# One-core decoder kernel: score order and copies in layer 3 cross attention, layer 0 FFN in chunks of four tiles, layer 2 routing in chunks

## The chip, the cores and the metric

The kernel runs on one core of a Trainium2 chip. The metric is the device time of one execution in microseconds (us), the median of several executions. The engines are TensorE (PE; its weight loads are shown as PEld), VectorE (DVE), ScalarE (ACT), GpSimd (POOL) and the queue of SyncE (SP).

## The reference

Four decoder layers, each of them self attention, cross attention and a feed forward part (FFN), each added to the residual x of 8 x 256 tokens by 128 features after a layer norm. The three parts that matter here:

```python
# layer 0 FFN
gate = jnp.einsum('bsd,hd->bsh', x, wg)      # 384 hidden features
up = jnp.einsum('bsd,hd->bsh', x, wu)
h = jax.nn.silu(gate) * up
return jnp.einsum('bsh,dh->bsd', h, wd)
...
# layer 2 FFN: 16 experts, two per token, 320 places in each
probs = jax.nn.sigmoid(xf @ gate_w.T)
top_vals, sel = jax.lax.top_k(probs, 2)
weights = top_vals / (top_vals.sum(-1, keepdims=True) + 1e-06)
flat_sel = sel.reshape(-1)
onehot = jax.nn.one_hot(flat_sel, 16, dtype=jnp.int32)
ranks = jnp.take_along_axis(jnp.cumsum(onehot, axis=0), flat_sel[:, None], axis=1)[:, 0] - 1
valid = ranks < capacity
slot = jnp.where(valid, flat_sel * capacity + ranks, sentinel)
padded = jnp.zeros((sentinel + 1, d), xf.dtype).at[slot].set(x_rep)
...
# layer 3 cross attention: q is the normalised x, k and v are the context, 16 heads of 8 features
scores = jnp.einsum('bhqd,bhkd->bhqk', qh, kh) + encoder_attention_mask
weights = jax.nn.softmax(scores, axis=-1)
ctx = jnp.einsum('bhqk,bhkd->bhqd', weights, vh)
return jax.nn.relu(ctx @ wo_w.T + wo_b)
```

## The kernel before

The residual lies in SBUF as 16 tiles of 128 tokens (NT = 16, two tiles per batch, TPB = 2, B = 8 batches). The stages follow one another in the order of the layers. A stage is a block: each engine runs its own list of instructions, written out by hand in program order, and waits on semaphores for the others. No engine enters the next block before all have left the last one. Nothing reorders the lists, so the order of the code sets the order of the work. All arithmetic is float32.

**Layer 0 FFN** is two blocks. `normalize_and_turn` (names L0n_...) is a loop over the 8 batches: DVE normalises two tiles into the one buffer `h`, PE transposes them into `psT`, ACT copies them to `part` and again to `hT`. `layernorm_scales` in front of it loads ACT's table and makes 1/std. `experts` (names L0f_...) is a loop over the 8 batches: PE multiplies gate and up weights with 256 tokens, two of the three blocks of 128 hidden features into one pair of PSUM banks and the third into another; ACT applies silu, DVE multiplies (`hidden`), PE multiplies with the down weights (`down`), DVE adds to x and takes the statistics for the next layer norm (`take_stats`).

**Layer 2 FFN** is three blocks. `turn_and_route` normalises in chunks of four tiles, transposes, and makes 16 logits per token. `slots_of_two` (names L2r_...) makes of all 16 tiles at once the sigmoid, the two best experts (`first_best`, twice), the count of tokens ahead of each (PE multiplies `count` with a triangular matrix and with ones; a chain of 15 small additions adds the tiles up in `ahead`) and the row number (`slot`) of each token and choice. `slot_experts` (names L2f_...) begins with 32 indirect DMAs from POOL's queue, two for each tile, that scatter the rows into the DRAM buffer `packed`; SP waits for all 32 and then loads the rows of the first pair of experts.

**Layer 3 cross attention** is `masked_heads` (names L3x_...). Its unit is an item: two heads times 128 queries times 256 keys, 16 items per batch, 128 in all. Four items are a group, and share one `score`: four products, one in each of four row strips of PE, into the four banks psS. Per item, DVE adds the mask and takes the row maximum (`reduce`, two instructions with a readout each), ACT takes the exponential (`exponent`, two instructions), PE transposes four 128x128 blocks into one of the two banks psE (`turn_exp`), and ACT or DVE copies them out (`keep`), as `by_dve(i)` says: every fourth by DVE. At the end of a batch PE multiplies with v (`weigh`, four parts), and in the next batch's items follow `keep_raw` (ACT), `spread_sums` (PE, row sums), `invert` (ACT, Ln and Exp), `divide` (POOL), `project` (PE) and `settle_x` (DVE). `score(g+1)` stands on PE before the transposes of the fourth item of group g (r == 3). `turn_exp(i)` waits for the copy of item i-2. On ACT the copy of item i-2 follows the exponential of item i.

## Time and profile before

| | |
|---|---|
| median of the timed executions | 1830.55 us (two others: 1828.64 and 4648.13) |
| the profiled execution | 1822.58 us, of which the span of the trace is 1820.9 us |
| PE busy | 1421.6 us, 78% |
| DVE busy | 851.2 us, 47% |
| ACT busy | 774.2 us, 43% |
| POOL busy | 430.0 us, 24% |
| mean granted TensorE clock | 0.899 of 2.4 GHz |

The busy shares are means over stages that differ much. The trace's times run from the start of the span. The three stages of the change lie at 416 to 490 us (layer 0 FFN), 1230 to 1405 us (layer 2 FFN) and 1451 to 1697 us (layer 3 cross attention). A float32 product shows as two MATMUL instructions in the trace, and a transpose as one.

### The profile page before, as it was taken

The page shows a single profiled execution, that of the slowest core. Times are in us where ns is not written, and L with a number is a line of the kernel's source. Part 1 is how long each engine was busy: PE and PEld are TensorE (multiplying, and loading weights), DVE is VectorE, ACT ScalarE, POOL GpSimd, SP SyncE. Part 2 cuts the span into 40 slices and gives each one's busy share as a digit, 9 for nine tenths or more (in the row PEclk, how much of TensorE's full clock was granted, in tenths as well). Part 3 has the DMA queues.
Part 4 walks back from the last instruction along what each step waited for, and adds up shares of the span by engine and source line. Part 5 has one row for each costly group of instructions (what it writes and reads, how often), then busy time and mean ns, then how long its engine had stood idle before and what let it go on. Part 6 is the DMA issues. An engine that isn't in the chain of part 4 may idle for free. (4 is left out here: it accounts for less than half of the span.)

```text
span 1820.9 us, 28110 instructions
## 1 busy us (share of the span) xinstructions
PE 1421.6 (78%) x10037; PEld 796.7 (44%) x10037; DVE 851.2 (47%) x2388; ACT 774.2 (43%) x1655; POOL 430.0 (24%) x512
## 2 busy tenths in 40 slices
PE   6899999994699999886997999872182668777585
PEld 4344444443544444464465344362161534344364
DVE  4555555533345655455113665354033545455432
ACT  3244444442167677551430233442020476767233
POOL 5543333300022110100003433001553222220034
PEclk9999999997999999896999999985596898898787
DMA  7900000000000000000004000000222000000022
GB/s 211 120 1 2 2 1 1 1 2 0 0 1 1 1 1 1 1 1 1 1 1 171 1 2 1 1 1 8 76 59 68 13 7 13 7 13 1 4 61 74
DMA packets 60253, 42.29 MB, mean 23 GB/s; under 512 B 13189, under 2 KB 54121, under 8 KB 60121
## 3 DMA queue, kind: packets, MB, share of 16 engines
q1 hardware_dynamic: 54752, 32.42, 7.2%
q0 software_dynamic: 3552, 7.33, 1.2%
q8 instruction: 80, 1.31, 0.3%
q10 hardware_dynamic: 1816, 0.81, 0.2%
q14 instruction: 53, 0.43, 0.1%
HBM read 25.88 MB, written 14.66 MB: 22 GB/s over the span
## 5 line engine op out<-in xcount | busy, mean ns | idle before, releaser
L927 ACT ACTIVATE L0a_probs<-L0a_psL 128x512 f32<-128x512 f32 x192 | 104.2, 594 | 203.5 <-PE L0a_psL L735 73.5
L1313 ACT ACTIVATE L3x_e<-L3x_e,L3x_neg_max 128x256 f32<-128x256 f32 x256 | 116.1, 504 | 69.0 <-DVE L3x_neg_max L1366 69.0
L1229 PE MATMUL L3x_psE<-ident,L3x_e 128*128 128x128 f32 x512 | 91.5, 308 | 61.5 <-ACT scores_L_experts_L L1321 59.3
L991 DVE TENSOR_REDUCE L0a_mx_part<-L0a_psS 128x4 f32<-128x512 f32 x120 | 77.3, 686 | 106.1 <-PE L0a_psS L678 81.8
L1366 DVE CUSTOM_DVE_ANT_0 L3x_e<-L3x_psS,L3x_mask_rows 128x256 f32<-128x256 f32 x256 | 90.9, 421 | 65.1 <-PE L3x_psS L1221 65.1
L1229 PEld LDWEIGHTS L3x_psE<-ident,L3x_e 128*128 128x128 f32 x512 | 61.5, 155 | 119.7 <-ACT L3x_e L1313 86.1
L580 POOL TENSOR_SCALAR L0a_km<-L0a_kT,quad_rows 128x256 f32<-128x256 f32 x64 | 58.4, 930 | 198.9 <-ACT L0a_kT L898 198.9
L670 PE MATMUL L0a_psS<-L0a_km,L0a_qT 32*128 32x512 f32 x360 | 102.2, 644 | 0.2 <-DVE L0a_mx_part L996 0.2
L927 ACT ACTIVATE L2a_probs<-L2a_psL 128x512 f32<-128x512 f32 x96 | 52.1, 594 | 104.2 <-PE L2a_psL L731 69.4
L704 PE MATMUL L0a_psL<-L0a_qm,L0a_kT 32*128 32x512 f32 x256 | 72.9, 643 | 21.8 <-DVE L0a_mx L991 20.3
L1565 PE MATMUL L1a_psL<-L1a_soft_near,neg_tri 128*128 128x512 f32 x128 | 67.9, 612 | 0.2 <-DVE L1a_soft_near L1772 0.2
L2847 POOL DMA_INDIRECT packed_rows<-h,slot x32 | 31.0, 967 | 142.8 <-POOLq L92 133.3
L1772 DVE TENSOR_TENSOR L1a_soft_near<-L1a_soft_near,L1a_psL 128x512 f32<-128x512 f32 x64 | 41.1, 684 | 41.4 <-ACT L1a_soft_near L1702 41.4
L1728 ACT ACTIVATE scores_L_experts_L<-L1a_psL 128x512 f32<-128x512 f32 x96 | 53.5, 594 | 12.8 <-PE L1a_psL L1569 12.8
L580 POOL TENSOR_SCALAR L0a_qm<-L0a_qT,quad_rows 128x256 f32<-128x256 f32 x64 | 58.0, 924 | 0.0
L1469 POOL TENSOR_SCALAR L1a_qm<-L1a_qT,quad_rows 128x256 f32<-128x256 f32 x32 | 29.0, 925 | 113.1 <-ACT L1a_qT L1683 113.1
L1321 ACT COPY scores_L_experts_L<-L3x_psE 128x512 f32<-128x512 f32 x96 | 54.6, 569 | 0.2 <-PE L3x_psE L1229 0.2
L991 DVE TENSOR_REDUCE L2a_mx_part<-L2a_psS 128x4 f32<-128x512 f32 x56 | 36.1, 686 | 35.7 <-PE L2a_psS L678 17.9
L991 DVE TENSOR_REDUCE L0a_mx<-L0a_psS 128x4 f32<-128x512 f32 x60 | 38.6, 685 | 29.2 <-PE L0a_psN L766 26.6
L2881 PE MATMUL L2f_psX<-ident,L2f_rows 128*128 128x128 f32 x40 | 6.9, 311 | 56.6 <-DMA L2f_rows<-packed_rows 55.4
L1163 POOL TENSOR_SCALAR L3x_km<-ctx_T,quad_rows 128x256 f32<-128x256 f32 x32 | 29.1, 925 | 89.3 <-POOLq L92 57.6
L2935 ACT ACTIVATE L2f_hidden<-L2f_psU 128x320 f32<-128x320 f32 x32 | 13.5, 437 | 85.1 <-PE L2f_psU L2891 68.9
(720 smaller groups left out, 3534.6 us busy)
## 6 DMA issues: line engine op xcount, KB each, us to landing
L2f_rows<-packed_rows SPq DMA_DIRECT2D x8, 325.0 KB
packed_rows<-zeros SPq DMA_DIRECT2D x1, 2560.0 KB, 27.8
experts_L_L<-in_L_ffn_w_dram SPq DMA_DIRECT2D x1, 2048.0 KB, 8.7
unpacked_rows<-zeros SPq DMA_DIRECT2D x1, 2048.0 KB, 17.7
scores_L_experts_L<-in_L_ffn_w_dram SPq DMA_DIRECT2D x1, 2048.0 KB, 8.2
L2f_back_rows<-unpacked_rows SPq DMA_DIRECT2D x16, 128.0 KB, 2.5
L3x_mask_rows<-in_mask_Bx1xSxS_ff_dram SPq DMA_DIRECT2D x8, 256.0 KB, 2.7
sorted_rows<-zeros SPq DMA_DIRECT2D x1, 1472.0 KB, 17.6
```

Source lines behind the costliest of these rows:

```text
L580: last = nc.gpsimd.tensor_scalar(dst[:, b % 3, j, :], src[:, b % 3, :], w["rows4"][:, j:j + 1], None, ALU.mult)
L670: last = nc.tensor.matmul(psS[a][:], qT[rows, b % 3, t * P:(t + 1) * P], km[rows, b % 3, :, u * P:(u + 1) * P], start=True, stop=of(b).mas ...
L704: nc.tensor.matmul(bank[:], kT[rows, b % 3, 0:P], qm[rows, b % 3, 2 * k:2 * k + 2, :], start=True, stop=False, skip_group_check=True)
L927: nc.scalar.activation(probs[:, half, a, k, :], psL[i % RING][:], ACT.Exp, scale=scale).then_inc(s_prob, 1)
L991: nc.vector.tensor_reduce(dst, psS[a][:].rearrange("p (j n) -> p j n", j=4), AX.X, ALU.max).then_inc(s_red, 1)
L1229: last = nc.tensor.transpose(psE[i % 2][:, c * P:(c + 1) * P], e[:, i % RING, c * P:(c + 1) * P], mem.ident[:])
L1313: last = nc.scalar.activation(at, at, ACT.Exp, bias=neg[:, i % RING, j:j + 1], scale=-1.0)
L1321: nc.scalar.copy(kept_at(i), turned(i)).then_inc(s_kept_act, 1)
L1366: last = nc.vector.tensor_tensor_reduce(out=e[:, i % RING, j * S:(j + 1) * S], in0=psS[r][:, j * S:(j + 1) * S], in1=mrow[:, b % 2, t, :], ...
L1565: last = nc.tensor.matmul(bank(s, a)[:], w["neg_tri"][:], soft(s, a), start=False, stop=kk == 0, skip_group_check=True)
L1728: nc.scalar.activation(probs[:, half, a, (kk + 2) % 3, :], bank(s, a)[:], ACT.Exp).then_inc(s_prob, 1)
L1772: nc.vector.tensor_tensor(soft(s, a), soft(s, a), bank(s, a)[:], ALU.max).then_inc(s_soft, 1)
```

## The change

In `masked_heads`, `score(g+1)` moves before the transposes of the third item (r == 2), which puts it also before the `weigh` that stands there. DVE copies every second item: item 4g+1 after the reduce of item 4g+3 as before, and item 4g+3 after the reduce of item 4g+4. `settle_x` moves from behind the last reduce of a batch to ahead of it (n == 14). `spread_sums` and `project` write psO in place of psM, and the waits change with that: the next batch's `weigh` waits for `settle_x`.

Layer 0's FFN is one block, `gated_ffn`, written out, with chunks of four tiles (512 tokens): every product has 512 columns, one block of hidden features per pair of banks, two normalised chunks ahead, and the down product of chunk c-1 between the products of chunk c. The wait for the late weights goes.

Layer 2's `turn_and_route` and `slots_of_two` become one block, `send_to_slots`, with chunks of four tiles, and the scatters move into it: POOL sends the eight scatters of a chunk as soon as its slots are ready. SP still waits for all 32, in the next block.

```diff
-        def by_dve(i):
-            return i % 4 == 1
-
         def wait_kept(eng, i):
-            if by_dve(i):
-                eng.wait_ge(s_kept_dve, i // 4 + 1)
+            if i % 2 == 1:
+                eng.wait_ge(s_kept_dve, i // 2 + 1)
             else:
-                eng.wait_ge(s_kept_act, i // 4 * 3 + (1, 0, 2, 3)[i % 4])
+                eng.wait_ge(s_kept_act, i // 2 + 1)
...
-                    if b >= 3:
-                        pe.wait_ge(s_ln, b - 2)
...
                     if r == 0:
                         if b >= 1:
-                            pe.wait_ge(s_raw, b)
+                            pe.wait_ge(s_x, b)
                         else:
                             pe.wait_ge(s_rows_kept, 1)
...
                 def spread_sums(b):
                     pe.wait_ge(s_raw, b + 1)
-                    pe.wait_ge(s_hT, min(b + 3, B))
-                    if b >= 1:
-                        pe.wait_ge(s_x, b)
-                    nc.tensor.matmul(psM[:], w["spread"][:], raw[:], start=True, stop=True).then_inc(s_den, 1)
+                    nc.tensor.matmul(psO[:], w["spread"][:], raw[:], start=True, stop=True).then_inc(s_den, 1)
 
                 def project(b):
                     pe.wait_ge(s_yT, b + 1)
-                    pe.wait_ge(s_hT, min(b + 4, B))
                     for t in range(TPB):
                         for a in range(2):
-                            last = nc.tensor.matmul(psM[:, t * P:(t + 1) * P], yT[:, a, t * P:(t + 1) * P], wo_rows[:, a, :],
+                            last = nc.tensor.matmul(psO[:, t * P:(t + 1) * P], yT[:, a, t * P:(t + 1) * P], wo_rows[:, a, :],
                                                     start=a == 0, stop=a == 1)
...
                         i = ITEMS * b + n
                         g, r = divmod(n, 4)
-                        if r == 3 and i + 1 < LAST:
+                        if r == 2 and i + 2 < LAST:
                             score(i // 4 + 1)
                         if n == 0 and b > 0:
...
                     exponent(i)
-                    if i >= 2 and not by_dve(i - 2):
+                    if i >= 2 and i % 2 == 0:
                         keep(i - 2)
...
                 keep(LAST - 2)
-                keep(LAST - 1)
...
                     reduce(i)
+                    if n % 4 == 0 and i > 0:
+                        keep(i - 1)
                     if n % 4 == 3:
                         keep(i - 2)
-                    if n == 15 and b > 0:
+                    if n == 14 and b > 0:
                         settle_x(b - 1)
+                keep(LAST - 1)
                 settle_x(B - 1)
 
...
+def gated_ffn(nc, mem, w, name, gate, up, down):
...
+                def expand(c, f):
+                    u = PARTS * c + f
+                    if f == 0:
+                        pe.wait_ge(s_hT, c + 1)
+                    if u >= 2:
+                        pe.wait_ge(s_hid, u - 1)
+                    at = slice(c * WIDE, (c + 1) * WIDE)
+                    nc.tensor.matmul(psG[u % 2][:], gate[:, f * P:(f + 1) * P], hT[:, at], start=True, stop=True)
+                    nc.tensor.matmul(psU[u % 2][:], up[:, f * P:(f + 1) * P], hT[:, at], start=True, stop=True).then_inc(s_up, 1)
+
+                def contract(c, tiles_of):
+                    pe.wait_ge(s_hid, PARTS * (c + 1))
+                    if c >= 2:
+                        pe.wait_ge(s_x, c - 1)
+                    for t in tiles_of:
+                        for f in range(PARTS):
+                            last = nc.tensor.matmul(psY[c % 2][:, t * D:(t + 1) * D], hid[:, c % 2, f, t * P:(t + 1) * P], down[:, f, :],
+                                                    start=f == 0, stop=f == PARTS - 1)
+                    if tiles_of[-1] == CHUNK - 1:
+                        last.then_inc(s_down, 1)
+
+                turn(0)
+                turn(1)
+                for c in range(CHUNKS + 1):
+                    if c < CHUNKS:
+                        expand(c, 0)
+                        expand(c, 1)
+                    if c >= 1:
+                        contract(c - 1, (0, 1))
+                    if c < CHUNKS:
+                        expand(c, 2)
+                    if c >= 1:
+                        contract(c - 1, (2, 3))
+                    if c + 2 < CHUNKS:
+                        turn(c + 2)
...
+                normal(0)
+                normal(1)
+                for c in range(CHUNKS + 1):
+                    if c < CHUNKS:
+                        hidden(c)
+                    if c + 2 < CHUNKS:
+                        normal(c + 2)
+                    if c >= 1:
+                        add(c - 1)
...
+def send_to_slots(nc, mem, w, name, gate, rows, packed, scattered, E, capacity):
...
+                for c in range(CHUNKS):
+                    pool.wait_ge(s_twin, c + 1)
+                    pool.wait_ge(s_slot, c + 1)
+                    for t in range(c * CHUNK, (c + 1) * CHUNK):
+                        for i in range(2):
+                            nc.gpsimd.indirect_dma_start(packed, bass.IndirectOffsetOnAxis(ap=slot[:, i, t:t + 1], axis=0),
+                                                         rows[:, i, t, :], None).then_inc(scattered, 16)
...
+                def rank_rows(c):
+                    pe.wait_ge(s_count, c + 1)
+                    if c >= 2:
+                        pe.wait_ge(s_slot, c - 1)
+                    nc.tensor.matmul(psK[c % 2][:, 0:CHUNK * E], w["earlier"][:], count[:], start=True, stop=True)
+                    nc.tensor.matmul(psK[c % 2][:, CHUNK * E:2 * CHUNK * E], w["ones"][:], count[:], start=True, stop=True).then_inc(s_ranked, 1)
+
+                route(0)
+                for c in range(CHUNKS):
+                    if c + 1 < CHUNKS:
+                        route(c + 1)
+                    rank_rows(c)
...
+                def choose(c):
+                    dve.wait_ge(s_exp, c + 1)
+                    steps.step(nc.vector.tensor_scalar(probs[:], probs[:], 1.0, None, ALU.add))
+                    steps.step(nc.vector.reciprocal(probs[:], probs[:]))
+                    best(probs, 0)
+                    steps.step(nc.vector.scalar_tensor_tensor(rest[:], one[:, 0, :, :], -2.0, probs[:], ALU.mult, ALU.add))
+                    best(rest, 1)
+                    if c >= 1:
+                        dve.wait_ge(s_ranked, c)
+                    nc.vector.tensor_tensor(count[:], one[:, 0, :, :], one[:, 1, :, :], ALU.add).then_inc(s_count, 1)
+                    steps.step(nc.vector.scalar_tensor_tensor(total[:], val[:, 0, :], 1e-6, val[:, 1, :], ALU.add, ALU.add))
+                    steps.step(nc.vector.reciprocal(total[:], total[:]))
+                    steps.step(nc.vector.tensor_tensor(val[:], val[:], total[:].unsqueeze(1).to_broadcast([P, 2, CHUNK]), ALU.mult))
...
+                def place(c):
+                    dve.wait_ge(s_ranked, c + 1)
+                    earlier = psK[c % 2][:, 0:CHUNK * E].rearrange("p (t e) -> p t e", e=E)
+                    counts = psK[c % 2][:, CHUNK * E:2 * CHUNK * E].rearrange("p (t e) -> p t e", e=E)
+                    for k in range(CHUNK):
+                        t = c * CHUNK + k
+                        steps.step(nc.vector.tensor_tensor(ahead[:, t + 1, :], ahead[:, t, :], counts[:, k, :], ALU.add))
+                    steps.step(nc.vector.tensor_tensor(equal[:], ahead[:, tiles(c), :], earlier, ALU.add))
+                    steps.step(nc.vector.tensor_tensor(both[:], one[:], equal[:].unsqueeze(1).to_broadcast([P, 2, CHUNK, E]), ALU.mult))
+                    steps.step(nc.vector.tensor_reduce(rank[:].unsqueeze(3), both[:], AX.X, ALU.add))
...
+                steps.step(nc.vector.memset(ahead[:, 0, :], 0.0))
+                normal(0)
+                normal(1)
+                for c in range(CHUNKS):
+                    choose(c)
+                    if c + 2 < CHUNKS:
+                        normal(c + 2)
+                    place(c)
...
-                pool.wait_ge(w["zeroed"], 16 * len(blanks(w)))
-                for t in range(NT):
-                    for i in range(2):
-                        nc.gpsimd.indirect_dma_start(packed, bass.IndirectOffsetOnAxis(ap=slot[:, i, t:t + 1], axis=0),
-                                                     rows[:, i, t, :], None).then_inc(s_scatter, 16)
...
-                sp.wait_ge(s_scatter, 16 * 2 * NT)
+                sp.wait_ge(scattered, 16 * 2 * NT)
...
-        with nc.sbuf_tensor("hT0", [P, NT * P], F32) as hT:
-            normalize_and_turn(nc, mem, w, "L0n", hT)
-            experts(nc, mem, w, "L0f", [(hT, w["L0_ffn_w_gate"][:], w["L0_ffn_w_up"][:], w["L0_ffn_w_down"][:], None)], ACT.Silu)
+        gated_ffn(nc, mem, w, "L0f", w["L0_ffn_w_gate"], w["L0_ffn_w_up"], w["L0_ffn_w_down"])
```

What stands in a row, in three places. First layer 0's FFN on PE. Before, the loop's body for one batch:

```order
L2354 MATMUL L0f_psG<-hT,wT_L_gate 128x256 x2
L2354 MATMUL L0f_psU<-hT,wT_L_up 128x256 x2
L2348 REGISTER_ALU
L2354 MATMUL L0f_psG<-hT,wT_L_gate 128x256
L2354 MATMUL L0f_psU<-hT,wT_L_up 128x256
L2335 REGISTER_ALU
L2336 REGISTER_ALU
L2340 MATMUL L0f_psY<-wT_L_down,L0f_hidden 128x128 x6
```

and now, from the third chunk's transposes on, one chunk's share (L2182 transposes, L2192 and L2193 are gate and up, L2201 is the down product):

```order
L2182 MATMUL L0f_psT<-ident,L0f_h 128x128 x4
L2192 MATMUL L0f_psG<-L0f_hT,wT_L_gate 128x512
L2193 MATMUL L0f_psU<-L0f_hT,wT_L_up 128x512
L2192 MATMUL L0f_psG<-L0f_hT,wT_L_gate 128x512
L2193 MATMUL L0f_psU<-L0f_hT,wT_L_up 128x512
L2201 MATMUL L0f_psY<-wT_L_down,L0f_hidden 128x128 x6
L2192 MATMUL L0f_psG<-L0f_hT,wT_L_gate 128x512
L2193 MATMUL L0f_psU<-L0f_hT,wT_L_up 128x512
L2201 MATMUL L0f_psY<-wT_L_down,L0f_hidden 128x128 x6
```

The products have 512 columns where they had 256, and the down product stands behind the products of the chunk after it.

Second, layer 2's routing on PE. Before, the last two chunks' transposes and logits and the ranking of all 16 tiles (psR of L2r):

```order
L2475 MATMUL L2n_psT<-ident,h 128x128 x4
L2484 MATMUL L2n_psR<-wT_r,L2n_hT 128x16 x8
L2445 UNCONDITIONAL_BRANCH
L2767 UNCONDITIONAL_BRANCH
L2770 MATMUL L2r_psR<-L2r_count,earlier 128x256
L2771 MATMUL L2r_psR<-L2r_count,ones 128x256
```

and now the first two chunks' transposes and logits, the ranking of the first chunk (psK), and the third chunk's:

```order
L2660 MATMUL L2n_psT<-ident,h 128x128 x4
L2665 MATMUL L2n_psR<-wT_r,L2n_hT 128x16 x4
L2660 MATMUL L2n_psT<-ident,h 128x128 x4
L2665 MATMUL L2n_psR<-wT_r,L2n_hT 128x16 x4
L2672 MATMUL L2n_psK<-L2n_count,earlier 128x64
L2673 MATMUL L2n_psK<-L2n_count,ones 128x64
L2660 MATMUL L2n_psT<-ident,h 128x128 x4
```

The ranking stands behind each chunk, with 64 columns, and no longer behind all of them, with 256.

Third, layer 3's cross attention on PE, two groups of a batch. Before (L1221 is score, L1229 the transposes, four for an item, L1208 the next q, L1260 project):

```order
L1221 MATMUL L3x_psS<-L3x_km,L3x_qT 128x512 x4
L1229 MATMUL L3x_psE<-ident,L3x_e 128x128 x4
L1208 MATMUL L3x_psM<-ident,L3x_h 128x128 x2
L1229 MATMUL L3x_psE<-ident,L3x_e 128x128 x12
L1221 MATMUL L3x_psS<-L3x_km,L3x_qT 128x512 x4
L1229 MATMUL L3x_psE<-ident,L3x_e 128x128 x4
L1260 MATMUL L3x_psM<-L3x_wo_rows,L3x_yT 128x128 x4
L1229 MATMUL L3x_psE<-ident,L3x_e 128x128 x12
L1221 MATMUL L3x_psS<-L3x_km,L3x_qT 128x512 x4
```

and now (L1174 is score, L1182 the transposes, L1161 the next q, L1209 project):

```order
L1174 MATMUL L3x_psS<-L3x_km,L3x_qT 128x512 x4
L1182 MATMUL L3x_psE<-ident,L3x_e 128x128 x8
L1161 MATMUL L3x_psM<-ident,L3x_h 128x128 x2
L1182 MATMUL L3x_psE<-ident,L3x_e 128x128 x8
L1174 MATMUL L3x_psS<-L3x_km,L3x_qT 128x512 x4
L1182 MATMUL L3x_psE<-ident,L3x_e 128x128 x8
L1209 MATMUL L3x_psO<-L3x_wo_rows,L3x_yT 128x128 x4
L1182 MATMUL L3x_psE<-ident,L3x_e 128x128 x8
L1174 MATMUL L3x_psS<-L3x_km,L3x_qT 128x512 x4
```

The score moved up past the transposes of one item. On DVE in the same place, the reduces of a group with the copy before (two ISA rows are half an item):

```order
L1366 ISA L3x_e,L3x_neg_max<-L3x_psS,L3x_mask_rows 128x256
L1366 ISA L3x_neg_max 128x1
L1366 ISA L3x_e,L3x_neg_max<-L3x_psS,L3x_mask_rows 128x256
L1366 ISA L3x_neg_max 128x1
L1366 ISA L3x_e,L3x_neg_max<-L3x_psS,L3x_mask_rows 128x256
L1366 ISA L3x_neg_max 128x1
L1376 COPY scores_L_experts_L<-L3x_psE 128x4x128
L1366 ISA L3x_e,L3x_neg_max<-L3x_psS,L3x_mask_rows 128x256
L1366 ISA L3x_neg_max 128x1
```

and now:

```order
L1314 ISA L3x_e,L3x_neg_max<-L3x_psS,L3x_mask_rows 128x256
L1314 ISA L3x_neg_max 128x1
L1324 COPY scores_L_experts_L<-L3x_psE 128x4x128
L1314 ISA L3x_e,L3x_neg_max<-L3x_psS,L3x_mask_rows 128x256
L1314 ISA L3x_neg_max 128x1
L1314 ISA L3x_e,L3x_neg_max<-L3x_psS,L3x_mask_rows 128x256
L1314 ISA L3x_neg_max 128x1
L1324 COPY scores_L_experts_L<-L3x_psE 128x4x128
L1314 ISA L3x_e,L3x_neg_max<-L3x_psS,L3x_mask_rows 128x256
L1314 ISA L3x_neg_max 128x1
```

A second copy (L1324) stands behind the first reduce of each group.

## Rows read from the trace of the kernel before

**Rows 1.** Windows: length; busy us (instructions) of PE, PEld, DVE, ACT, POOL; clock; DMA; GB/s.
```profile
416.00:437.00 21.00, 5.28 (x16) 2.32 (x16) 6.81 (x16) 8.02 (x19) 0.00 (x0) 0.50 0.00 0
437.00:490.00 53.00, 35.32 (x192) 29.61 (x192) 20.52 (x64) 9.13 (x17) 0.00 (x0) 0.95 0.00 0
1230.00:1267.00 37.00, 12.44 (x52) 11.03 (x52) 21.46 (x65) 8.54 (x14) 0.00 (x0) 0.50 0.00 0
1267.00:1309.00 42.00, 0.00 (x0) 0.00 (x0) 0.00 (x0) 0.66 (x1) 30.95 (x32) 0.50 0.15 51
...
1451.00:1697.00 246.00, 180.89 (x1374) 102.29 (x1374) 123.85 (x586) 167.00 (x384) 48.48 (x61) 0.89 0.03 7
```

**Rows 2.** Timeline, layer 0 FFN's normalise stage: start, us, engine, what; [idle before].
```profile
416.05 1.28 ACT L128 ACT_TABLE_LOAD   x1 [4.32 <-PEq L92]
...
435.97 0.40 ACT L2289 COPY hT<-L0n_hT_part 128x256 f32 x1 [0.19 <-ACT L0n_hT_part L2286]
```

**Rows 3.** Timeline, layer 0 FFN, its last batch.
```profile
481.81 1.03 PE L2354 MATMUL L0f_psU<-hT,wT_L_up 128*128 x4
...
484.24 1.02 DVE L2408 TENSOR_TENSOR L0f_hidden<-L0f_activated,L0f_psU 128x512 f32<-128x512 f32 x2 [0.50 <-ACT L0f_activated L2375]
...
485.50 1.58 PE L2340 MATMUL L0f_psY<-wT_L_down,L0f_hidden 128*128 128x128 f32 x12 [1.80 <-DVE L0f_hidden L2408]
...
489.53 0.17 DVE L154 COPY mean_var<-bn_aggr 128x4 f32 x1 [0.24 <-DVE bn_aggr L152]
```

**Rows 4.** Timeline, layer 1 attention: one product with 512 columns, full clock.
```profile
571.50 1.02 PE L1565 MATMUL L1a_psL<-L1a_soft_near,neg_tri 128*128 128x512 f32 x2
```

**Rows 5.** Timeline, layer 2 routing and the first load behind it.
```profile
1232.75 0.69 DVE L2465 TENSOR_TENSOR h<-h,rstd 128x512 f32<-128x512 f32 x1 [1.15 <-ACT rstd L2451]
...
1235.73 1.73 PE L2484 MATMUL L2n_psR<-wT_r,L2n_hT 128*128 128x16 f32 x8
...
1247.32 1.75 DVE L2778 RECIPROCAL L2r_probs<-L2r_probs 128x256 f32<-128x256 f32 x1
...
1254.14 0.42 DVE L2782 TENSOR_TENSOR L2r_count<-L2r_onehot 128x256 f32<-128x256 f32 x1
...
1254.62 1.22 PE L2770 MATMUL L2r_psR<-L2r_count,earlier 128*128 128x256 f32 x2 [10.54 <-DVE L2r_count L2782]
...
1262.90 0.17 DVE L2806 TENSOR_SCALAR slot<-L2r_at 128x16 uint32<-128x16 f32 x1
...
1308.94 7.68 SPq L2861 DMA_DIRECT2D L2f_rows<-packed_rows  x5
```

**Rows 6.** The 32 scatters into packed_rows: ns min/median/max, first and last start.
```profile
L2847 POOL DMA_INDIRECT packed_rows<-h,slot x32: 957/962/1173, 1267.1 to 1306.6; - x32
```

**Rows 7.** Timeline, layer 3 routing: a DVE product beside a scatter.
```profile
1724.77 2.49 DVE L3268 TENSOR_TENSOR h<-h,L3f_score 128x512 f32<-128x512 f32 x4
1726.29 1.30 POOL L3059 DMA_INDIRECT sorted_rows<-h,L3f_slot  x1 [30.44 <-DVE h L3268]
```

**Rows 8.** Layer 3 cross attention grouped by line: busy, mean ns, idle before.
```profile
L1313 ACT ACTIVATE L3x_e<-L3x_e,L3x_neg_max 128x256 f32<-128x256 f32 x256 | 116.1, 504 | 69.0 <-DVE L3x_neg_max L1366 69.0
...
L1321 ACT COPY scores_L_experts_L<-L3x_psE 128x512 f32<-128x512 f32 x96 | 54.6, 569 | 0.2 <-PE L3x_psE L1229 0.2
...
L1376 DVE COPY scores_L_experts_L<-L3x_psE 128x512 f32<-128x512 f32 x32 | 22.1, 692 | 54.6 <-PE L3x_psE L1229 54.6
```

**Rows 9.** The score products of layer 3 cross attention.
```profile
L1221 PE MATMUL L3x_psS<-L3x_km,L3x_qT x256: 587/692/1218, 1451.2 to 1680.8; 32*128 32x512 f32 x128
```

**Rows 10.** Timeline, one group of four items and the next score.
```profile
1546.32 1.14 PE L1221 MATMUL L3x_psS<-L3x_km,L3x_qT 32*128 32x512 f32 x8
...
1547.62 0.42 DVE L1366 CUSTOM_DVE_ANT_0 L3x_e<-L3x_psS,L3x_mask_rows 128x256 f32<-128x256 f32 x1 [2.08 <-PE L3x_psS L1221]
...
1548.43 0.91 ACT L1313 ACTIVATE L3x_e<-L3x_e,L3x_neg_max 128x256 f32<-128x256 f32 x2 [2.62 <-DVE L3x_neg_max L1366]
...
1554.01 1.18 PE L1221 MATMUL L3x_psS<-L3x_km,L3x_qT 32*128 32x512 f32 x8
```

405 lines of the change are left out of this document (148 added, 257 removed).

## The prediction

> **What bounds the kernel now.** I read the windows by stage first, because the shares of the whole span mix stages with different limits, then the timeline inside each stage, and last the grouped lines of the cross attention. [rows 1] is to show that in none of the three stages an engine is full. In layer 0's first 21 us PE is busy for 5.3 and ACT for 8.0; each loop step is a chain of DVE, PE, ACT with nothing beside it, and the granted clock is 0.50, the 1.2 GHz level. In the 53 us behind it PE is busy for 35.3 at 0.95. In layer 2, 37 us pass in which DVE is busy for 21.5 and POOL not at all, and then 42 us in which only POOL works: the 32 scatters go out one after another, from 1267.1 to 1306.6 [rows 6], which is 39.5/31 = 1.27 us each, and nobody else has work. In the cross attention PE is busy for 181 of 246 us, ACT for 167, DVE for 124. There the grouped lines show 69.0 us in which ACT waited for DVE's reduces [rows 8], and a group's timeline shows why: score at 1546.32, first reduce at 1547.62, first exponential at 1548.43, with 2.62 us idle ahead of it [rows 10]. So ACT and DVE sit idle at each group's start because PE begins the score late. All three stages lie on the path to the end, since blocks follow one another.
>
> **Layer 0 FFN.** Now it takes from 416.05 [rows 2] to 489.7 [rows 3], 73.65 us. I lay the new block out. The table load (1.28), Ln and Exp end at about 417.9; one normalising product over four tiles is 0.69 [rows 5], so the first chunk is ready at 418.7. Four transposes take about 1.1 at half clock, two chunks of them until 421.3, the second chunk's normalising keeping pace. One product of 512 columns is two instructions in 1.02 with about 0.17 of pipe [rows 4], so 0.85 in a row, and a gate and up pair 1.7. The first pair runs at half clock (3.0 with the change of clock in it), the others at 1.7: the first chunk is through at 428. From there PE's work in a chunk is three pairs (5.1), twelve down products (two times 1.4, from 1.58 for six [rows 3] less the pipe) and four transposes (0.6): 8.5 us. There is one new wait. DVE normalises chunk c+2 only behind the last `hidden` of chunk c, and PE's transposes of c+2 stand ahead of the next pair: silu 0.6 and its hop 0.2, product 0.7 and normalising 1.4 make 2.9 to 3.3 after the third pair, of which the down products cover 1.3 where there are any. That costs 3.2 us once and 1.9 once. The last chunks need 8.5 each, and the tail (down products, sum, statistics of four tiles) some 4 us. The end comes at about 464.6, so **this part gives 25 us**. It can't be more than 30 (PE's work alone, 34, with start and tail 9), and if the first two chunks stay at half clock, which costs 5 more, it is 20. DVE (about 5.8 per chunk) and ACT (2.4) are hidden below PE. If that cover went, DVE would be next; it has 2.7 us left per chunk.
>
> **Layer 2 routing.** The path to the first load at 1308.94 [rows 5] is: everything for all tiles, then all scatters. In the new block the first chunk is normalised by 1233.44 as now, its logits need transposes and half of the eight instructions' 1.73 and a copy [rows 5], so the exponential ends at about 1237.4. DVE's operations for 64 elements lie between 0.17 (16 elements) and 0.42 (256) [rows 5]; by the line between these about 0.22, with the step 0.26. `choose` is 13 of them, a reciprocal (1.75 for 256, about 0.55 for 64) and three tiny ones: 4.6. PE's ranking (1.22 and 1.06 for 256 columns now) is hidden by the 1.4 of the next chunk's normalising. `place` is four tiny additions and about nine small steps: 2.9. The first slots are there at about 1246.3, where now the first scatter starts at 1267.1. From there the scatters decide: 8 x 1.27 = 10.1 us per chunk, and DVE needs 4.6 + 1.4 + 2.9 = 8.9 for the next. With 32 in a row the last one ends at 1287.2, 20.3 us earlier. SP's wait for them stands now behind the end of a block, which costs 1.7 after the last scatter (as between the last slot and the first scatter now) in place of 1.4: **20 us gained**. The bound above is 21. For the bound below I price 64 elements like 256: DVE then needs 15 us per chunk and is the bound, the last slots come at 1295 and the scatters end at 1305, which leaves 3. I take the first, since the small operations' own rows lie near it. ACT's second copy of the rows and the table load for Gelu, 1.28, now wait for the block's end, but the load and the transposes of 3 us and more cover it.
>
> Here a contention is thinkable, since DVE now works beside the scatters. In the trace a DVE product with both inputs in SBUF (four of them, 2.49 us in all, three steps of 0.60 and one of 0.69) runs beside a scatter that starts at 1726.29 [rows 7], and none of the four is longer than without one. The Trainium skill says in "SBUF — State Buffer", section "Who interferes with whom", that such an instruction contends with a GpSimd instruction that reads SBUF, and that one of the two then blocks for the whole instruction. By that rule some 18 of this gain's 20 us would go (the second rival prices it) and the sum be 51 in place of 69; by the row nothing goes, and I go by the row.
>
> **Layer 3 cross attention.** 32 scores start between 1451.2 and 1680 [rows 9], so a group takes 7.4 us. The cycle without extras: score to first reduce 1.30, reduce to exponential 0.81 [rows 10], three items on ACT of 1.28 each (0.81 exponential, 0.47 copy), 0.1, then the transposes of the third item 0.57 and the next score: 6.6. With the batch's extras (weigh on PE, the copies, Ln and Exp on ACT) such a layout gives 27.9 per batch of four groups, where the trace has 29.6; the difference I put to stretches at half clock, the mean being 0.89 [rows 1]. After the change the third exponential is no longer in the way, and one copy of two has left ACT. The new cycle goes through DVE: score 1.07, transposes of the two items left over 1.14, then DVE's copy of the fourth item 0.69 [rows 8], which stands ahead of the second reduce, the reduce 0.81, the exponential 0.93, the transposes 0.57: 5.3 with the hops. The wait for all four reduces stands in the same place: 1.3 + 0.69 x 5 = 4.8 after the score, and later when the copy waited. In the group of `settle_x` it stands ahead of the last reduce and adds 1.9, to 7.2. The extras of PE and ACT add about 1 us to each of the other three. A batch is then 6.3 + 6.3 + 6.3 + 7.2 = 26.1, the first, without extras, 20.5. That would be 7 x 3.5 + 7.2 = 32 us gained, if the half clock went away; with its present loss of 1.7 per batch it is 19. PE is denser afterwards, so I take a value between, **24 us**. The bounds are 8 (waits for copies eat most of it) and 35. Off ACT go 32 copies of 0.57 [rows 8], onto DVE come 32 of 0.69, 22 us in all; DVE's 124 of 246 become about 146 of 222 and stay hidden. The psO in place of psM removes waits that came early, and costs nothing: `settle_x` is done a group before the `weigh` that waits for it.
>
> **The sum** is 25 + 20 + 24 = 69 us. The profiled execution took 1822.6 with its span of 1820.9, and 1822.6 - 69 = 1753.6. The timed ones have a median of 1830.5, 8 us above it, and the forecast is made for that: **1761.5 us**, 3.8% faster. Since DMA in these stages is light, I expect nothing given back later.
>
> **The rivals.** *First: the new wait eats the earlier score.* The score can't start before the group's four reduces, and DVE now has two copies and `settle_x` among them, each waiting on PE. If the group stays at 7.4, the cross attention gives nothing: 1830.5 - 45 = 1785.5. For it: DVE waited 54.6 us for its present 32 copies [rows 8]. Against it: these waits fell where DVE had no reduce to do.
> *Second: contention in layer 2.* Some 18 of DVE's operations per chunk have two inputs in SBUF. If each waited 0.4 us on average for a scatter (0.96 busy in 1.27), DVE's chunk would take 16 us against 10.1, three times, and 18 of the 20 us are lost: 1779.5. The Trainium skill's rule above speaks for it, [rows 7] against it.
> *Third, and slower than before: the clock.* PE's 181 busy us in the cross attention at 0.89 are 322 at 0.50 [rows 1], 76 more than the 246 it has. If PE stood at the 1.2 GHz level through the stage, it would lose that and the whole be 1830.5 - 45 + 76 = 1861. It decides from a mean clock of about 0.65 there, at which PE's need alone (161 / 0.65) passes 246, and from 0.55 (161 / 0.55 = 293) it outweighs the other 45. Against it: PE's work is packed closer, and 0.89 is far off.
> *Fourth: the change does more than forecast.* With no half clock in the cross attention and 28 from layer 0 it is 1830.5 - 28 - 21 - 33 = 1748.5.
>
> **How the numbers follow.** The forecast, with its own range of 1752 to 1775, gets 0.62; the first rival 0.14; the second 0.04; the third 0.01; the fourth 0.13; what is left, 0.06, is several shortfalls at once. A measurement here tells about 2%, 37 us, from no change, so faster than 1794 counts as faster. The range reaches from the fourth (with 6 us for the scatter between executions, 1742) to the first (1787); outside lie the third, the mixtures, and the half of the first in which other terms fall short too, about 0.14. Faster by over 2%: 0.96. Within 2%: 0.03, a shortfall of two parts at once. Slower: 0.01.
>
> **What the new profile would show.** Layer 0's stage some 48 us long, PE's clock at 1 from its first chunk on, PE waiting twice for the normalising. The first scatter at about 16 us after the block's start instead of 36, 32 scatters without a gap over 0.4 us between chunks, and DVE's 64-element steps near 0.22. Score starts 6.3 to 6.6 us apart, 7.2 in the group with `settle_x`, ACT's wait for reduces well below 69 us, and a clock above 0.89. What would make me wrong is a period of over 7 us, gaps between the scatters' chunks, or PE at half clock through layer 0.

## The result and the profile after

The changed kernel took a median of 1762.2 us (four executions, 1759.7 to 1763.1) where the kernel before took 1830.7 (1828.6 to 1830.8, and one execution of 4648.1 that no ratio uses), a ratio of 0.9627 with a 95% interval of 0.9608 to 0.9646: 68.5 us less, 3.7% faster. Its profiled execution took 1761.7 us with a span of 1760.0, at a mean clock of 0.908.

The forecast was 1761.5 us, 0.7 off. But the two profiled executions are only 60.9 us apart, where I had summed 69. The profiled execution of the kernel before lay 8 us below its median, that of the changed one 0.5 below. So the sum fell 8 us short of what the profiles show, and my adding 8 us back covered that by luck. By block, between the loads of ACT's table that begin them: layer 0's FFN went from 74.5 to 47.6 (27.0 gained, forecast 25); layer 2's FFN from 175.3 to 161.4 (13.9, forecast 20); layer 3's cross attention from 255.0 to 230.7 (24.3, forecast 24); and the unchanged stages between layers 1 and 2 together 3.9 us longer, which I had at nothing.

The windows of the changed kernel by stage (length; busy us of PE, PEld, DVE, ACT, POOL; clock; DMA share; GB/s), for [rows 1]:

```profile
415.63:431.80 16.17, 10.60 (x27) 5.59 (x28) 6.04 (x9) 6.64 (x10) 0.00 (x0) 0.71 0.00 0
431.80:463.20 31.40, 26.46 (x135) 17.75 (x133) 15.16 (x47) 5.97 (x10) 0.00 (x0) 0.99 0.00 1
1207.40:1223.50 16.10, 9.91 (x40) 8.35 (x40) 11.20 (x40) 5.55 (x11) 0.24 (x1) 0.50 0.01 2
1223.50:1272.90 49.40, 6.39 (x25) 5.28 (x24) 19.28 (x90) 1.55 (x4) 30.96 (x32) 0.50 0.13 43
1407.70:1638.40 230.70, 172.94 (x1382) 98.35 (x1382) 147.18 (x624) 156.86 (x357) 53.62 (x67) 0.92 0.03 10
```

In layer 0, PE is busy for 26.5 of the last 31.4 us. In layer 2 the first scatter goes out 16.2 us after the block's start, as laid out, but from there to SP's load it takes 49 us where the working had 42. The cross attention's clock rose from 0.89 to 0.92 and DVE's busy time to 147 us, as forecast.

PE in layer 0's new block, its first products and its two waits for the normalised rows:

```profile
420.49 1.63 PE L2192 MATMUL L0f_psG<-L0f_hT,wT_L_gate 128*128 128x512 f32 x2
421.96 1.02 PE L2193 MATMUL L0f_psU<-L0f_hT,wT_L_up 128*128 128x512 f32 x2
...
429.15 1.12 PE L2182 MATMUL L0f_psT<-ident,L0f_h 128*128 128x128 f32 x4 [2.73 <-DVE L0f_h L2253]
...
440.39 0.66 PE L2182 MATMUL L0f_psT<-ident,L0f_h 128*128 128x128 f32 x4 [1.40 <-DVE L0f_h L2253]
```

The granted clock leaves the 1.2 GHz level at 421.7, inside the first pair. It is back there from 428.5 to 431.9, beginning inside the wait of 2.73 us, and four transposes take 1.12 us where they take 0.66 behind the second wait.

The timeline of the changed kernel shows what was missing in layer 2. Rows of DVE in its fourth chunk, and then of POOL and SP:

```profile
1238.97 0.18 DVE L2750 SCALAR_TENSOR_TENSOR L2n_slot<-L2n_at,token 128x8 uint32<-128x8 f32 x1
...
1241.23 0.22 DVE L2715 TENSOR_TENSOR L2n_equal<-L2n_probs,L2n_val 128x64 f32<-128x64 f32 x1 [0.47 <-issue]
1241.93 0.22 DVE L2716 TENSOR_TENSOR L2n_equal<-L2n_equal,desc 128x64 f32<-128x64 f32 x1 [0.48 <-DVE L2n_equal L2715]
1242.63 0.22 DVE L2717 TENSOR_REDUCE L2n_key<-L2n_equal 128x4 f32<-128x64 f32 x1 [0.47 <-DVE L2n_equal L2716]
...
1253.16 0.17 DVE L2740 TENSOR_TENSOR L2n_ahead<-L2n_ahead,L2n_psK 128x16 f32<-128x16 f32 x1 [1.24 <-DVE L2n_ahead L2740]
1254.56 0.17 DVE L2740 TENSOR_TENSOR L2n_ahead<-L2n_ahead,L2n_psK 128x16 f32<-128x16 f32 x1 [1.22 <-DVE L2n_ahead L2740]
...
1258.69 0.17 DVE L2750 SCALAR_TENSOR_TENSOR L2n_slot<-L2n_at,token 128x8 uint32<-128x8 f32 x1
1259.62 0.96 POOL L2649 DMA_INDIRECT packed_rows<-h,L2n_slot  x1 [5.79 <-DVE L2n_slot L2750]
...
1268.47 0.96 POOL L2649 DMA_INDIRECT packed_rows<-h,L2n_slot  x1 [0.30 <-issue]
1272.92 1.51 SPq L2809 DMA_DIRECT2D L2f_rows<-packed_rows  x3
```

Each instruction takes as long as in the chunks before (0.22 for 64 elements), but they start 0.70 or 1.40 us apart in place of 0.26. So the fourth chunk took 19.7 us, where the second and third took 8.6 and 8.0, and POOL waited 5.8 us. The profile names no other engine in these gaps, only DVE's own instruction before. A late load of code doesn't show either: between 1223 and 1284 us the trace has no packet of the instruction queues. The last gap of 0.70 us begins at 1256.66, when the 24th scatter, the last one sent by then, has been over for 2.8 us. And SP's load starts 3.5 us behind the last scatter's end, where I had 1.7.

The grouped lines of the changed kernel's cross attention, in a rerun of it (e5 below), for [rows 8]; columns as there:

```profile
L1262 ACT ACTIVATE L3x_e<-L3x_e,L3x_neg_max 128x256 f32<-128x256 f32 x256 | 112.4, 499 | 54.0 <-DVE L3x_neg_max L1314 53.2
L1324 DVE COPY scores_L_experts_L<-L3x_psE 128x512 f32<-128x512 f32 x64 | 44.2, 691 | 41.7 <-PE L3x_psE L1182 40.8
L1174 PE MATMUL L3x_psS<-L3x_km,L3x_qT 32*128 32x512 f32 x256 | 40.9, 711 | 9.6 <-DVE L3x_neg_max L1314 9.0 <-ACT L3x_qT L1256 0.6
L1270 ACT COPY scores_L_experts_L<-L3x_psE 128x512 f32<-128x512 f32 x64 | 36.0, 563 | 0.0
```

ACT's wait for the reduces fell from 69.0 to 53.2 only, and the score now waits for DVE, 9.0 us in all, which it did not before.

### The profile page after: what moved, and what is told of

Same layout as the page of the kernel before. It is cut to its first block and busy times, and to the rows that moved or that the text cites. A ratio compares the mean times of both kernels' runs of the same rounds, so it can differ in the third digit from the quotient of the medians.

```text
span 1760.0 us, 27583 instructions
## 1 busy us (share of the span) xinstructions
PE 1415.8 (80%) x10001; PEld 785.2 (45%) x10001; DVE 875.7 (50%) x2460; ACT 756.1 (43%) x1609; POOL 430.4 (24%) x513
## 5 line engine op out<-in xcount | busy, mean ns | idle before, releaser
L1262 ACT ACTIVATE L3x_e<-L3x_e,L3x_neg_max 128x256 f32<-128x256 f32 x256 | 112.4, 499 | 55.8 <-DVE L3x_neg_max L1314 55.2
L949 DVE TENSOR_REDUCE L0a_mx_part<-L0a_psS 128x4 f32<-128x512 f32 x120 | 77.3, 686 | 105.6 <-PE L0a_psS L636 81.3
L1182 PE MATMUL L3x_psE<-ident,L3x_e 128*128 128x128 f32 x512 | 84.3, 297 | 38.6 <-ACT L3x_e L1262 25.1
L628 PE MATMUL L0a_psS<-L0a_km,L0a_qT 32*128 32x512 f32 x360 | 101.4, 640 | 0.2 <-DVE L0a_mx_part L954 0.2
L1182 PEld LDWEIGHTS L3x_psE<-ident,L3x_e 128*128 128x128 f32 x512 | 58.6, 149 | 87.2 <-ACT L3x_e L1262 68.3
L1324 DVE COPY scores_L_experts_L<-L3x_psE 128x512 f32<-128x512 f32 x64 | 44.3, 691 | 42.0 <-PE L3x_psE L1182 41.4
L1174 PE MATMUL L3x_psS<-L3x_km,L3x_qT 32*128 32x512 f32 x256 | 42.0, 728 | 9.6 <-DVE L3x_neg_max L1314 9.0
L628 PE MATMUL L2a_psS<-L2a_km,L2a_qT 32*128 32x512 f32 x168 | 49.0, 660 | 0.2 <-DVE L2a_mx_part L954 0.2
L2800 POOL DMA_INDIRECT unpacked_rows<-L2f_y,L2f_ids x40 | 38.4, 960 | 41.9 <-DVE L2f_y L2904 31.3
L2470 DVE SCALAR_TENSOR_TENSOR scores_L_experts_L<-L1f_psB,slot_column,L1f_gates_wide 128x256 f32<-128x256 f32 x32 | 15.5, 484 | 64.6 <-ACT L1f_gates_wide L2578 64.6
```

The source lines that it names most:

```text
L628: last = nc.tensor.matmul(psS[a][:], qT[rows, b % 3, t * P:(t + 1) * P], km[rows, b % 3, :, u * P:(u + 1) * P], start=True, stop=of(b).mas ...
L949: nc.vector.tensor_reduce(dst, psS[a][:].rearrange("p (j n) -> p j n", j=4), AX.X, ALU.max).then_inc(s_red, 1)
L1174: nc.tensor.matmul(psS[r][:], qT[rows, b % 3, t * P:(t + 1) * P], km[rows, b % 2, 2 * pair:2 * pair + 2, :], start=True, stop=True).then_i ...
L1182: last = nc.tensor.transpose(psE[i % 2][:, c * P:(c + 1) * P], e[:, i % RING, c * P:(c + 1) * P], mem.ident[:])
L1262: last = nc.scalar.activation(at, at, ACT.Exp, bias=neg[:, i % RING, j:j + 1], scale=-1.0)
L1324: nc.vector.tensor_copy(kept_at(i), turned(i)).then_inc(s_kept_dve, 1)
```

## The experiments

All were timed against the kernel before, in three groups (e1 to e4, e5 to e8, e9 to e12), on other chips or at other times than the pair above; there it takes 1804.5 to 1805.2 us, 26 less. Where that lies is told at the end. Differences are taken inside a group, or between groups by the ratios.

**e1 to e3: each part alone.** The kernel before, with only `gated_ffn`, only `send_to_slots` (with its scatters), or only the new `masked_heads`.

> The kernel before with layer 0's chunked FFN alone. In the two profiles that block is 26.9 us shorter (490.6 - 416.05 against 463.2 - 415.6), while the stages between layer 1 and layer 2, whose code is the same, were 3.8 us longer. Theory A, those 3.8 us are chance (where PE's half-clock stretches fall from one execution to another): the median is 26 to 28 us below the kernel before. Theory B, the shorter block pushes the phase of the clock into the stages behind it, and 3 to 4 us of the gain are given back each time: 22 to 24 us below.

> The kernel before with layer 2's chunked routing alone. The profile after shows 13.9 us for it where I forecast 20: DVE's fourth chunk took 19.7 us in place of 8.6, POOL waited 5.8 us for its slots, and the load began 3.5 us after the last scatter in place of 1.7. Theory A, this belongs to the block itself: the time is 13 to 15 us below the kernel before and the fourth chunk is slow again, from the 13th scatter on. Theory B, it came from where the program stood at that moment (the code before it is another here): the fourth chunk takes under 11 us and the gain is 18 to 20 us.

> The kernel before with layer 3's cross attention alone. Forecast 24, in the profiles 24.3 (255.0 to 230.7 us). Theory A, the profiled executions of both kernels are typical there: 23 to 26 us below. Theory B, the kernel before loses more to half clock in its timed executions than in its profiled one, which would be where the 8 us between its profile and its median come from: 30 us below or more, and the three parts alone add up to the 68.5 us of the medians.

Measured against 1804.7: e1 1775.4 (0.9844, 0.9822 to 0.9867), e2 1786.5 (0.9905, 0.9882 to 0.9927), e3 1774.4 (0.9829, 0.9809 to 0.9850): 29.3, 18.2 and 30.3 us, each to about 4. For e1, A is nearer: nothing is given back (the unchanged stages between layers 1 and 2 are 2 us shorter in its trace than in those of e2 and e3). For e2, B: the fourth chunk took 8.1 us and 32 scatters went out without a gap. For e3, B: the unchanged cross attention took 259.1 and 262.4 us in the traces of e1 and e2, and only in the profiled execution of the kernel before 255.0. Its windows in e2 show the clock at 0.84 in place of 0.89:

```profile
1426.50:1688.90 262.40, 193.98 (x1401) 111.22 (x1400) 127.69 (x584) 168.76 (x385) 43.20 (x56) 0.84 0.02 7
```

**e4: no scatter beside DVE's work.**

```diff
-                    pool.wait_ge(s_slot, c + 1)
+                    pool.wait_ge(s_slot, CHUNKS)
```

> The changed kernel, but no scatter is sent before the last chunk's slots are ready; the block is otherwise the same. Theory A, the scatters slow DVE down in the fourth chunk: without them beside it every chunk of DVE takes 8.6 us, the last slots come at 36 + 12 = about 43 us after the block's start less the first 8, that is at about 40 us (51.3 in the changed kernel), and the scatters then end 41 us later, so that the whole is 15 to 18 us slower than the changed kernel, 1777 to 1780 us. Theory B, the slow fourth chunk is DVE's own (its code, not the scatters): it takes 19 us again, the last slots stay at 51 us and the whole is 26 to 29 us slower than the changed kernel, about 1790 us.

1752.8 us (0.9720, 0.9698 to 0.9743), by the ratios 22 us slower than the changed kernel in e5. DVE's last instruction for the slots of the four chunks started 15.06, 23.60, 31.56 and 39.52 us after the block's start, as theory A has it; the scatters started at 40.6. But e5 has 15.06, 23.61, 31.58 and 39.53 with the scatters beside them. In the seven other experiments with the changed block and all scatters beside it, the last of the four comes at 39.6 to 39.7. So where the stall was absent the scatters cost DVE at most 0.2 us in three chunks, and this run, right by A's number, doesn't show A.

**e5: the changed kernel again; e6: DVE's list shifted; e7: half the scatters in the next block.** e6:

```diff
                 normal(1)
+                for k in range(32):
+                    nc.vector.memset(filler[:, k:k + 1], 0.0)
```

e7 (`slot` is kept for the next block, whose first instructions on POOL are the scatters of tiles 8 to 15):

```diff
-                for c in range(CHUNKS):
+                for c in range(CHUNKS // 2):
                     pool.wait_ge(s_twin, c + 1)
```

> The changed kernel once more, on a chip where the kernel before takes about 1804.7 us if it is the one of the last four runs. There the parts alone gave 29, 18 and 30 us, 78 together. Theory A (the slow fourth chunk of DVE came from where the program stands, since it was absent with layer 2's part alone): it comes again, the routing block takes 65 to 66 us up to SP's load and the whole is 72 us below the kernel before, 1733 us. Theory B (it belonged to that one execution or chip): the block takes 60 us and the whole is 78 us below, about 1727 us.

> The changed kernel with 32 one-element writes on DVE in the routing block, between the second chunk's normalising and the wait for the first exponential (2.7 us of idle time there, the writes need about 2). They move all of DVE's later instructions of the block by 32 places, about one chunk. Theory A (the stall hangs on a place in DVE's instruction list, reached while scatters run): the stretch of 0.7 us steps starts one chunk earlier, at about 24 us into the block, and POOL waits for the third chunk's slots in place of the fourth's; the loss is 5 to 15 us. Theory B (it hangs on the number of scatters sent): it starts at the 13th scatter again, 31.6 us into the block. Theory C (chance): no stall, the block takes 60 to 61 us.

> The changed kernel, with the last two chunks' 16 scatters moved behind the end of the routing block, to the start of the next one, ahead of SP's wait as in the kernel before. Theory A: the 3.4 us between the last scatter and SP's load are the end of the block behind POOL's last scatter; here the load comes 1.4 us behind the last scatter and the block's end falls beside DVE's fourth chunk, where POOL loses no more than 1 to 3 us; with a fourth chunk of DVE of 8 us the load comes at 58 to 60 us after the block's start, the same as or up to 2 us earlier than in the changed kernel without a stall, and 6 us earlier than with it. Theory B: the 3.4 us are the time in which the last rows land, and stay: the load at 60 to 62 us, the whole 1 to 2 us slower.

Against 1805.2: e5 1731.5 (0.9597, 0.9576 to 0.9618), e6 1729.5 (0.9582, 0.9563 to 0.9600), e7 1732.1 (0.9592, 0.9574 to 0.9611). In e5 the stall is gone, though the program is the same, so it doesn't come from the place in the program; the load starts 60.1 us after the block's start (65.5 with the stall). Therefore e6, whose block takes 59.9, says only that 32 small writes in idle time cost nothing. By the whole time B isn't confirmed: 73.7 us gained (69.0 to 76.5 by the ratio) is nearer to A's 72 than to B's 78, which was a sum of three parts known to 4 us each. It is the timeline that decides for B. DVE's last slots come at 39.5 us, and the load at 60.1. DVE in e5, in the same chunk and beside the same scatters:

```profile
1237.54 0.22 DVE L2714 TENSOR_REDUCE L2n_val<-L2n_probs 128x4 f32<-128x64 f32 x1
1237.80 0.22 DVE L2715 TENSOR_TENSOR L2n_equal<-L2n_probs,L2n_val 128x64 f32<-128x64 f32 x1
1238.05 0.22 DVE L2716 TENSOR_TENSOR L2n_equal<-L2n_equal,desc 128x64 f32<-128x64 f32 x1
```

e7 was right on the wait and wrong on its price. POOL and SP there:

```profile
1241.14 1.01 POOL L2649 DMA_INDIRECT packed_rows<-h,slot  x1 [0.30 <-issue]
1246.92 0.96 POOL L2799 DMA_INDIRECT packed_rows<-h,slot  x1 [4.77 <-POOLq L92]
...
1265.86 0.96 POOL L2799 DMA_INDIRECT packed_rows<-h,slot  x1 [0.30 <-issue]
1268.16 1.51 SPq L2813 DMA_DIRECT2D L2f_rows<-packed_rows  x3
```

With the end of the block out of the way the load follows 1.3 us behind the last scatter, so of the 3.4 us of the changed kernel 2.1 are the block's end, and the rest is there without it too. But the block can't end before DVE's fourth chunk, at 39.7 us, and POOL is idle for 4.8 us there: load at 62.4 in place of 60.1.

**e8: the earlier score, without the second copy on DVE.**

```diff
+        def by_dve(i):
+            return i % 4 == 1
...
-                    if n % 4 == 0 and i > 0:
-                        keep(i - 1)
```

> The changed kernel, but in layer 3's cross attention DVE copies every fourth item as before, and the score still comes ahead of the third item's transposes. Theory A (the earlier score made the gain, and the second copy on DVE stands in its way, since reduces and so the next score wait behind it): groups of 5.9 to 6.2 us, a mean below 6.5, and the whole 5 to 12 us faster than the changed kernel. Theory B (ACT would be the bound again, three copies of 0.57 and four exponentials of 0.81 are 5.0 of ACT per group plus the extras): a mean of 6.6 to 7.0 and 3 to 15 us slower.

1713.1 us (0.9499, 0.9476 to 0.9521), 18 us faster than the changed kernel. The stage took 215.2 us in place of 230.6, its undisturbed groups 6.13, 5.95, 5.78 and 5.92 us. A was right, and gave it too little. Three of the lines shown for e5:

```profile
L1265 ACT ACTIVATE L3x_e<-L3x_e,L3x_neg_max 128x256 f32<-128x256 f32 x256 | 115.3, 503 | 29.6 <-DVE L3x_neg_max L1318 29.6
L1273 ACT COPY scores_L_experts_L<-L3x_psE 128x512 f32<-128x512 f32 x96 | 54.6, 569 | 0.5 <-PE L3x_psE L1185 0.5
L1177 PE MATMUL L3x_psS<-L3x_km,L3x_qT 32*128 32x512 f32 x256 | 40.7, 709 | 2.8 <-DVE L3x_neg_max L1318 2.3 <-ACT L3x_qT L1259 0.6
```

ACT works 18.6 us more on copies, and waits 23.6 less for the reduces.

**e9: the score late, both copies on DVE. e10: `settle_x` behind the last reduce.**

```diff
-                        if r == 2 and i + 2 < LAST:
+                        if r == 3 and i + 1 < LAST:
```

```diff
-                    if n == 14 and b > 0:
+                    if n == 15 and b > 0:
                         settle_x(b - 1)
```

> The changed kernel, but in layer 3's cross attention the next group's score stands ahead of the fourth item's transposes, as in the kernel before; DVE still copies every second item. With the earlier score and a copy on DVE for every fourth item the stage took 215 us, with both changes 231, with neither 255 to 262 in three profiles. Theory A (the earlier score makes the whole gain and the second copy on DVE only costs): this version takes 262 us or more there, groups of 7.4 us and above, and the whole is 30 us or more slower than the changed kernel. Theory B (each of the two gains by itself, the second copy by 0.57 us per group off ACT's path, and they only get in each other's way together): groups of 6.9 to 7.1 us and 14 to 20 us slower.

> The changed kernel with settle_x behind the last reduce of a batch again. Theory A (ahead of it, it holds up the fourth reduce, and so the next score, by some 0.7 to 1.9 us a batch; the fourth group of a batch is 6.98 us where the others are 6.13 to 6.28): that group falls to about 6.3, 7 times 0.7 are 5 us faster. Theory B (it stands then ahead of the next batch's first reduce and copy, and delays these as much): the first group grows by what the fourth loses, and the whole stays within 2 us.

Against 1804.5: e9 1752.1 (0.9719, 0.9699 to 0.9739), the stage 252.7 us, groups of 7.30 on average. That lies between the theories: with the late score the second copy does gain something (252.7 against 255.0, 259.1 and 262.4 in three traces with the old order), with the early one it costs. e10 1722.2 (0.9547, 0.9531 to 0.9563), the stage 219.8, twice what A gave. The place, in e5 and with the next score:

```profile
1455.69 1.09 PE L1182 MATMUL L3x_psE<-ident,L3x_e 128*128 128x128 f32 x8
...
1470.49 0.42 DVE L1330 TENSOR_TENSOR L3x_proj<-L3x_psO,L3x_out_bias 128x256 f32<-128x256 f32 x1
...
1470.95 0.42 DVE L1332 SCALAR_TENSOR_TENSOR x_resid<-L3x_proj,x_resid 128x256 f32<-128x256 f32 x1
...
1471.41 0.49 DVE L1335 BATCH_NORM_STATS2 bn_stats<-x_resid 128x6 f32<-128x128 f32 x2
...
1471.93 0.25 DVE L1338 BATCH_NORM_AGGREGATE mean_var<-bn_stats 128x2 f32<-128x6 f32 x2
1472.21 0.42 DVE L1314 CUSTOM_DVE_ANT_0 L3x_e<-L3x_psS,L3x_mask_rows 128x256 f32<-128x256 f32 x1
...
1473.04 1.14 PE L1174 MATMUL L3x_psS<-L3x_km,L3x_qT 32*128 32x512 f32 x8 [1.50 <-DVE L3x_neg_max L1314]
...
1474.11 1.97 PE L1182 MATMUL L3x_psE<-ident,L3x_e 128*128 128x128 f32 x8
```

The score waits 1.50 us for the fourth reduce, which stands behind `settle_x`; so six times in e5, 9.0 us, and never in e10. Here the granted clock is at the 1.2 GHz level from 1474.1 on, for 3.4 us: eight transposes take 1.97 us in place of the 1.09 behind an earlier score (the first row), and the group 7.70 us in place of 6.13. In e10 a batch is 6.90 + 6.16 + 6.28 + 5.41, 24.75 us against 25.55, which makes 5.6 in seven batches; and up to the last score there are two such stretches in place of five, each worth some 1.5 us. Together that is 10 of the 10.8. Theory B's first half was seen as well (the first group grows from 6.13 to 6.90), but the fourth loses more.

**e11: layer 0 normalises earlier. e12: the best of all together.**

```diff
                         nc.vector.tensor_tensor(hid[:, c % 2, f, :], ...
+                        if f == 1 and c + 2 < CHUNKS:
+                            normal(c + 2)
...
-                    if c + 2 < CHUNKS:
-                        normal(c + 2)
```

> The changed kernel; in layer 0's FFN DVE normalises chunk c+2 ahead of the third `hidden` of chunk c in place of behind it. Theory A (PE's two waits of 2.7 and 1.4 us for the normalising are on the path and go): 3 to 4 us faster, and PE keeps full clock through the third chunk's transposes, up to 2 us more. Theory B (DVE's 1.4 us then hold up the third `hidden`, which the pair of products two further on and the down products wait for, and PE waits there): within 1 us of the changed kernel.

> The earlier score with a copy on DVE for every fourth item, settle_x behind the last reduce of a batch, and the earlier normalising in layer 0. By the one before (1713.1 us with the first of the three) less 3 to 4 for the normalising, if theory A of that run holds: 1709 us; with settle_x moved, which has one copy fewer beside it here, 0 to 4 less: 1705 to 1710 us. If both moves give nothing, 1713 us.

e11 1724.7 (0.9556, 0.9540 to 0.9572), e12 1709.6 (0.9469, 0.9450 to 0.9488). e11's block takes 44.0 us in place of 49.0. In e5 PE's waits for the normalised rows are

```profile
PE L0f_psT L2182 <- DVE L0f_h L2253: 9.4, 4, 5.0
```

(in all, times, the longest, which is the start) and in e11

```profile
PE L0f_psT L2182 <- DVE L0f_h L2253: 6.2, 3, 5.0
```

so 3.2 us of waits have gone. The 3.4 us stretch at the 1.2 GHz level behind the first of them, which e5 has too, is also gone. With PE busy through it, I estimate that at half its length, 1.7 us: together 4.9 of the 5.0, as A has it. By the ratios the whole is 7 us faster, more than the block, but the two intervals allow 5 us either way. e12 is by the ratios 23 us faster than the changed kernel, and 95 us (5.3%) faster than the kernel before, inside what was expected. Its stages are 44.0 and 214.7 us, so nearly all that it has over e8 is layer 0's; with one copy per group on DVE the place of `settle_x` is worth no more than the 0.5 us between 215.2 and 214.7.

## Why the forecast held, and where it did not

**Layer 0 FFN: right, with a slip in the sum.** 25 forecast; 27 in the first profiles, 29.3 alone (about 4 either way), 25.5 in the block itself in e1. The terms as I gave them (the first chunk through at 428, three chunks of 8.5, waits of 3.2 and 1.9, a tail of 4) add up to 462.6, not to 464.6, so the working stood for 27. The block ended at 463.2. The two new waits were 2.73 and 1.40 us, and e11 shows that they were on the path. PE was at half clock in the first pair, as laid out; the 3.4 us of half clock behind the first wait were not in the sum. In e1 and e5 the half clock at the start reaches 2.2 us further into the block, and the block takes 49.0 us in place of 47.6.

**Layer 2 routing: the mechanism right, two terms of the sum off.** The first slots at 15.1 and the first scatter at 16.2 us came as laid out, DVE's chunk took 8.0 to 8.6 against my 8.9, and from there on the scatters followed one another without a gap, in all the experiments that keep this order. "SP's wait for them stands now behind the end of a block, which costs 1.7 after the last scatter" was too small: 3.4, of which e7 puts 2.1 on the block's end. So the load comes 18.0 us earlier than before in e5, in place of 20. In the first profile it came only 12.5 us earlier; the other 5.5 are the stall, which I hadn't in the sum. It left the gap between the scatters' chunks, 5.8 us, that the prediction named as a sign of being wrong.

The second rival, contention, doesn't explain it. DVE's products with both inputs in SBUF took 0.22 us with and without scatters, and e4 and e5 differ by 0.01 us after four chunks. Even in the stalled chunk they took 0.22; what grew was the time between them. And my row for it [rows 7] had the durations only. The Trainium skill's rule ("SBUF — State Buffer", "Who interferes with whom") was given only in part in the prediction. The same section adds, as an inference, that `tensor_tensor` takes only the read side of the shared pair of ports and that descriptor generation needs the write side. By that the descriptor work of a scatter would not hold up these products, and the 0.22 us agree with it.

Twenty us behind that row, the trace of before has a late start in layer 3, beside the last scatters there:

```profile
1743.29 1.02 PE L3091 MATMUL L3f_psU<-hT,experts_L_L 128*128 128x512 f32 x2
...
1748.04 0.60 ACT L3176 ACTIVATE L3f_act_out<-L3f_psG 128x512 f32<-128x512 f32 x1 [8.31 <-DMA L2f_back_rows<-unpacked_rows]
```

ACT's silu needs only these products and its bank, and came after 8.3 us of idle time, 2.4 us behind the start of the last scatter (1745.60). The sign stood in the trace that I read, and I looked at how long instructions take and not at how far apart they start.

**Layer 3 cross attention: the size right, the account wrong.** 24 forecast, 24.3 in the profiles; 30.3 alone, since the unchanged stage took 259.1 and 262.4 us in e1 and e2, with 66 and 68 us at the 1.2 GHz level between its first and its last score, against 255.0 with 52 in the execution that I had. The bounds were 8 and 35. The undisturbed groups were 6.13, 6.16, 6.28 and 6.98 us by my 6.3, 6.3, 6.3 and 7.2, so the cycle through DVE was laid out rightly, with the copy's 0.69 us in it and `settle_x` in the fourth group. Wrong was what I made of it: I counted the second copy as a gain, and never laid out the earlier score without it. The wait of the first rival, the new one that eats the earlier score, is there, but it eats a third of that gain and not all. The earlier score with the old copies gains 44 to 47 us (e8 against the unchanged stage), and the second copy takes 15.3 back (e5 against e8). With `settle_x` behind the last reduce the copy costs 5.1 (e10 against e12). `settle_x` ahead of the last reduce costs 10.8 where the second copy is there (e5 against e10). The half clock was the right thing to leave open: between the first and the last score it was 52 us before, 25 after and 15 in e12.

**The sum.** 1753.6 was forecast for a profiled execution, and it took 1761.7. Layer 2 gave 6.1 less: its load came 7.5 us later than laid out (5.5 for the stall, 1.7 for the block's end), and the experts behind it took 1.4 less than in the profile before. The unchanged stages between layers 1 and 2 took 3.9 us more. The largest piece of that is layer 2's self attention, 210.3 us where it took 207.4, with PE at the 1.2 GHz level for 15.7 us in place of 9.4; it takes 207.3 to 207.4 in every trace of the experiments. Layer 0 gave 2 more. That the median was met to 0.7 us is luck, two errors of 8 us that cancel: this one, and the base. I added the kernel before's 8 us between profile and median back as if the changed kernel had them too, and it has 0.5. e1 and e2 show that a profiled execution can lie 4 to 7 us off in the cross attention alone.
